# A drain behind each group of matmuls carries the semaphore update, in a four-layer graph attention kernel

## The reference

```python
def layer(x, adj, W, a, slope, bias, elu):
    wh = x @ W                                        # 4096 x 64
    e = (wh @ a[:64])[:, None] + (wh @ a[64:])[None, :]
    e = jnp.where(e > 0, e, slope * e)                # leaky relu
    att = jax.nn.softmax(jnp.where(adj > 0, e, -big), axis=1)
    h = att @ wh + bias                               # bias in layer 1 alone
    return layernorm(x + (jax.nn.elu(h) if elu else h))
```

## Time and profile before

| what | value |
|---|---|
| timed executions, median (lowest to highest) | 600.63 us (600.36 to 600.85) |
| span of the profiled execution, first to last instruction | 859.9 us |
| TensorE matmuls, busy | 419.1 us, 3453 instructions |
| TensorE weight loads, busy | 334.5 us |
| ScalarE, busy | 400.8 us |
| VectorE, busy | 349.6 us |
| GpSimd, busy | 278.0 us |
| granted TensorE clock, mean | 0.815 |

### The profile page before, as it was taken

One profiled execution on the slowest core, in us unless ns is written; L12 is line 12 of the kernel. 1 busy time (PEld: TensorE's weight loads), 2 busy tenths in 40 slices (PEclk: granted clock), 3 DMA queues, 4 the chain that ended last, 5 costly groups with the idle time before them and its releaser, 6 DMA issues.

```text
span 859.9 us, 10681 instructions
## 1 busy us (share of the span) xinstructions
PE 419.1 (49%) x3453; PEld 334.5 (39%) x3453; DVE 349.6 (41%) x1601; ACT 400.8 (47%) x876; POOL 278.0 (32%) x296
## 2 busy tenths in 40 slices
PE   2354512246655786411129983310499633104985
PEld 1243301245543675300119862210397522004964
DVE  3035813744379598200003872300048622000587
ACT  2677612555476476200325971231269612313684
POOL 0000173140320410777710034777100437771000
PEclk9999999999999998555559995755599857555997
DMA  8999962482673100222200012222000112220000
GB/s 312 428 330 428 422 198 58 173 290 100 212 282 124 17 26 27 32 27 27 27 8 2 20 30 29 28 27 27 9 1 20 34 26 27 28 28 6 8 19 28
DMA packets 20546, 84.86 MB, mean 99 GB/s; under 512 B 6083, under 2 KB 11462, under 8 KB 16262
## 3 DMA queue, kind: packets, MB, share of 16 engines
q1 hardware_dynamic: 10102, 73.15, 21.8%
q0 software_dynamic: 9344, 9.89, 9.4%
q10 hardware_dynamic: 1040, 1.08, 0.4%
HBM read 78.72 MB, written 5.37 MB: 98 GB/s over the span
## 4 chain that ended last, share of the span: by engine, by line
another core or an unknown queue 23%; PE 17%; DVE 12%; ACT 11%; issue 9%; DVEq 0%; ACTq 0%
PE bank L709 7%; ACT arena L865 4%; PE bank L689 3%; PE bank L672 3%; ACT arena L851 2%; DVE x L1313 2%; PE bank L670 1%; DVE stats L1295 1%; PE bank L705 1%; ACT arena L875 1%; DVE arena L1232 1%; ACT arena L839 1%; PE bank L574 1%; DVE res L1292 1%
## 5 line engine op out<-in xcount | busy, mean ns | idle before, releaser
L528 POOL DMA_INDIRECT xg<-table,index x292 | 277.8, 951 | 499.4 <-DMA table<-wh 299.8
L1232 DVE CUSTOM_DVE_ANT_0 arena<-bank,arena 128x256 f32<-128x256 f32 (+3 forms) x123 | 63.4, 523 | 284.7 <-ACT arena L851 224.5
L851 ACT ACTIVATE arena<-bank,sloped_own 128x256 f32<-128x256 f32 (+3 forms) x123 | 68.5, 557 | 176.3 <-remote 109.7
L689 PE MATMUL bank<-packed,arena 128*128 128x128 f32 x339 | 68.3, 323 | 120.0 <-issue 74.0
L839 ACT ACTIVATE arena<-arena,half 128x4096 bf16<-128x4096 int32 x31 | 114.7, 3703 | 19.1 <-DMA arena<-in_adj_t 18.5
L689 PEld LDWEIGHTS bank<-packed,arena 128*128 128x128 f32 x339 | 46.0, 165 | 132.7 <-issue 118.5
L875 ACT COPY arena<-bank 128x256 f32<-128x256 f32 (+3 forms) x123 | 54.1, 446 | 75.4 <-remote 55.4
L670 PE MATMUL bank<-off_row,wall 128*128 128x256 bf16 (+3 forms) x132 | 43.9, 332 | 81.2 <-issue 58.4
L709 PE MATMUL bank<-xg,arena 128*128 128x64 f32 x486 | 73.0, 284 | 10.6 <-ACT arena L875 8.6
L709 PEld LDWEIGHTS bank<-xg,arena 128*128 128x128 f32 x486 | 63.7, 197 | 24.0 <-ACT arena L875 13.5
L1029 DVE MAX8 top<-bank 128x8 f32<-128x256 f32 x31 | 13.4, 431 | 131.5 <-remote 69.5
(11 more groups left out here) (148 smaller groups left out, 780.1 us busy)
## 6 DMA issues: line engine op xcount, KB each, us to landing
arena<-in_adj_t SPq DMA_DIRECT2D x31, 2048.0 KB
xg<-table,index POOLq DMA_INDIRECT x292
table<-wh SPq DMA_DIRECT2D x24, 132.0 KB, 1.7
arena<-in_adj SPq DMA_DIRECT2D x1, 2048.0 KB, 12.9
table<-wh ACTq DMA_DIRECT2D x1, 1056.0 KB
x<-in_x SPq DMA_DIRECT2D x1, 1024.0 KB, 15.0
out_x<-x SPq DMA_DIRECT2D x8, 128.0 KB, 1.9
packed<-in_c_packed SPq DMA_DIRECT2D x1, 312.0 KB
```

Source lines behind the costliest of these rows:

```text
L528: pool.indirect_dma_start(out=xg[:, c, :], out_offset=None, in_=table[l][0:rows, :], in_offset=bass.IndirectOffsetOnAxis(ap=index[:, c:c + ...
L689: t = nc.tensor.transpose(turned_ps[turned_bank(n)][:, c * P:(c + 1) * P], scores(l, n)[:, c * P:(c + 1) * P], ident[:, :])
L851: nc.scalar.activation(scores(l, n)[:, 0:m * P], score_ps[n % len(score_ps)][:, 0:m * P], ACT.Relu, bias=sloped_own[:, k:k + 1], scale=ALP ...
L1232: nc.vector.tensor_tensor_reduce(out=y, in0=score_ps[n % len(score_ps)][:, 0:m * P], in1=y, scale=-1.0, scalar=-FLOOR, op0=ALU.add, op1=AL ...
```

## The change

In ten places of TensorE's program the matmul no longer carries the update of the group. A drain of TensorE is placed behind the group, and the drain carries it. The groups, their order, the waits in front of them, and everything on the other engines stay as they are. The transposes and products of the one-off preparation (lines 589 and 591), the overflow check and the branch for dense graphs keep their updates on the matmul.

```diff
@@ turn_rows
-                t.then_inc(xt_made, 1)
+                pe.drain().then_inc(xt_made, 1)
@@ project_rows
-                t.then_inc(wh_made, 1)
+                pe.drain().then_inc(wh_made, 1)
@@ sum_rows
                 nc.tensor.matmul(wh_ps[:, 0:F], x_total[:, :].broadcast_to([2 * F, P]), wx[:, l, 0:F],
-                                 start=True, stop=True).then_inc(sum_made, 1)
+                                 start=True, stop=True)
+                pe.drain().then_inc(sum_made, 1)
@@ pack
-                ins.then_inc(codes_made, 1)
+                pe.drain().then_inc(codes_made, 1)
@@ first_slots
-                t.then_inc(off_made, 1)
+                pe.drain().then_inc(off_made, 1)
@@ lists
-                    t.then_inc(list_made, 1)
+                    pe.drain().then_inc(list_made, 1)
@@ spread
                 for c in range(m):
-                    t = nc.tensor.matmul(bank[:, c * P:(c + 1) * P],
+                    nc.tensor.matmul(bank[:, c * P:(c + 1) * P],
                                          tcol_wide(terms[:, c1 + c, TCOL:TCOL + 1]), ident[:, :],
                                          start=False, stop=(c == m - 1), is_transpose=True)
-                t.then_inc(score_made, 1)
+                pe.drain().then_inc(score_made, 1)
@@ turn
-                t.then_inc(turned, 1)
+                pe.drain().then_inc(turned, 1)
@@ aggregate
-                t.then_inc(aggregated, 1)
+                pe.drain().then_inc(aggregated, 1)
```

More of the change, by code:

```diff
@@ L563, in turn_rows @@
                     k, at = g * GROUP + 2 * j, (n % 2 * PAIRS + j) * P
-                    t = nc.tensor.transpose(xt_ps[:, at:at + P],
+                    nc.tensor.transpose(xt_ps[:, at:at + P],
                                             x[:, k:k + 2, :].rearrange("p k f -> p (k f)"), ident[:, :])
-                t.then_inc(xt_made, 1)
+                pe.drain().then_inc(xt_made, 1)
             def project_rows(n, l, dst=wh_ps):
@@ L573, in project_rows @@
                 for j in range(PAIRS):
-                    t = nc.tensor.matmul(dst[:, 2 * j * WX:2 * (j + 1) * WX], xt[:, n % 2, j * P:(j + 1) * P],
+                    nc.tensor.matmul(dst[:, 2 * j * WX:2 * (j + 1) * WX], xt[:, n % 2, j * P:(j + 1) * P],
                                          wx_pair[:, l, :, :].rearrange("p a f -> p (a f)"), start=True, stop=True)
-                t.then_inc(wh_made, 1)
+                pe.drain().then_inc(wh_made, 1)
             def sum_rows(l):
@@ L605, in pack @@
                 for c in range(TILES):
-                    ins = nc.tensor.matmul(codes[:, c * w:(c + 1) * w], masks[:, t % 2, c * P:(c + 1) * P],
+                    nc.tensor.matmul(codes[:, c * w:(c + 1) * w], masks[:, t % 2, c * P:(c + 1) * P],
                                            packer[:, :], start=False, stop=(c == TILES - 1))
-                ins.then_inc(codes_made, 1)
+                pe.drain().then_inc(codes_made, 1)
             def first_slots(b):
@@ L616, in first_slots @@
                 pe.wait_ge(deg_made, b + 1)
-                t = nc.tensor.matmul(room_ps[:, 0:n], before[:, :], degb[:, 0:n], start=True, stop=True)
+                nc.tensor.matmul(room_ps[:, 0:n], before[:, :], degb[:, 0:n], start=True, stop=True)
                 if k0 < PARTED:
                     nc.tensor.matmul(room_ps[:, n:2 * n], before[:, :], degb[:, n:2 * n], start=True, stop=False)
-                    t = nc.tensor.matmul(room_ps[:, n:2 * n], ones_b[:, :], degb[:, 0:n], start=False, stop=True)
-                t.then_inc(off_made, 1)
+                    nc.tensor.matmul(room_ps[:, n:2 * n], ones_b[:, :], degb[:, 0:n], start=False, stop=True)
+                pe.drain().then_inc(off_made, 1)
             def lists(b):
@@ L640, in lists @@
                             high = k < PARTED and place < HIGH_TO[k]
-                            t = nc.tensor.matmul(dst, off_row[:, at:at + P], rows, start=False,
+                            nc.tensor.matmul(dst, off_row[:, at:at + P], rows, start=False,
                                                  stop=(k == tiles[-1] and not high))
@@ L646, in lists @@
                                 nc.tensor.matmul(dst[:, w - 1:w], ones_b[:, :], less, start=False, stop=False)
-                                t = nc.tensor.matmul(dst[:, w - 1:w], off_high[:, at:at + P], less,
+                                nc.tensor.matmul(dst[:, w - 1:w], off_high[:, at:at + P], less,
                                                      start=False, stop=(k == tiles[-1]))
-                    t.then_inc(list_made, 1)
+                    pe.drain().then_inc(list_made, 1)
             def spread(l, q):
@@ L688, in turn @@
                 for c in range(m):
-                    t = nc.tensor.transpose(turned_ps[turned_bank(n)][:, c * P:(c + 1) * P],
+                    nc.tensor.transpose(turned_ps[turned_bank(n)][:, c * P:(c + 1) * P],
                                             scores(l, n)[:, c * P:(c + 1) * P], ident[:, :])
-                t.then_inc(turned, 1)
+                pe.drain().then_inc(turned, 1)
             def aggregate(l, q):
@@ L708, in aggregate @@
                 for c in range(m):
-                    t = nc.tensor.matmul(agg[:, at:at + F], slots(l, n)[:, c * P:(c + 1) * P],
+                    nc.tensor.matmul(agg[:, at:at + F], slots(l, n)[:, c * P:(c + 1) * P],
                                          wh[:, c0 + c, 0:F] if k == DENSE else xg[:, FIRST[k] + c0 + c, 0:F],
```

## The result

The changed kernel takes 924.89 us (median of 4 runs, 923.14 to 926.07) against 600.74 us of the kernel before: 1.538 times as long, with a 95% interval of 1.535 to 1.542. The forecast was 706 us, with a range from 632 to 790.

What follows compares the result with a forecast made beforehand. TensorE was taken to bound the burst, with gathers close as a bound. Drains would add 89 us in layers 1 to 3, 13 in layer 0 and 3 ahead of it: 600.6 + 105 = 706 us, range 632 to 790.

Steps and rivals of the forecast that it cites:

- The clock, the rival that was given 0.07: Bursts of layers 1 to 3: TensorE's clock falls to 1.2 GHz, some 33 us more a layer, 805 us; chance 0.07.
- the sum: Whole kernel: drain costs less slack, 89 us in layers 1 to 3, 13 + 3 before, 706 us; chance 0.74.
- against it: Argument against the clock rival: clock 1.00 throughout the light rounds, with weight loads in 21.14 of 27.50 us.
- b: Cost of one drain between two TensorE groups without a gap: 0.34 us, from 0.17 to 0.50.
- The estimate by the 12 ns: One drain on TensorE taken at 12 ns: b would be 0.28 us, the sum some 22 us less.
- The slack of the rounds: Rounds from 460.7 to 505.0 us: slack between 1.3 and 8.3 us, taken as 4.8, set against 88 drains.
- Layer 0: From 290 to 343 us, some 80 drains less 14 us of slack cost 13 us; drains ahead of 290 us, 3.
- the long releases: ScalarE starts 11 us after line 672 while gathers are issued; taken as the profiler's, hardly present in timed executions.
- Gathers cover it: Timed layers bound by the gathers' pace, hiding 20 us of drains a layer: 646 us; chance 0.11.
- Faster by releases that are no longer held: Matmul updates are held while gathers are issued, a drain's are not: 555 us at best, about 580 with half; chance 0.05.
- Nothing changes: The last matmul's update already comes so late that a drain between groups adds nothing: 601 us; chance 0.03.
- The sign of a clock under 0.9: In the profile after, a clock under 0.9 from 453 us to the burst's end would speak for the clock rival.

Runs made afterwards that it cites:

- single kinds: Kernel before with only one of aggregates (line 709), turns (line 689) or spreads (lines 670, 672) drained: 642.43, 627.85 and 625.31 us.
- two kinds: Kernel before with turns and aggregates drained: 824.93 us, 775.44 with repeated matmuls added; with spreads and aggregates drained: 830.57 us.
- the new trace: The kernel before, unchanged, run once more with a profile: 602.71 us, span 600.8 us.
- aggregates alone: Kernel before with only the 164 updates of the aggregates (line 709) carried by a drain: 642.43 us.
- turns alone: Kernel before with only the 164 updates of the turns (line 689) carried by a drain: 627.85 us.
- spreads alone: Kernel before with only the 164 updates of the spreads (lines 670 and 672) carried by a drain: 625.31 us.
- layer 0 alone: Drains only in the listing and in layer 0, 204 of 609, the rest as in the kernel before: 660.17 us.
- the fill without drains: Kernel before, no drains, each transpose of a turn done twice and a spread's first matmul three times, into the same place: 653.29 us.

## Why the prediction failed

**The clock, the rival that was given 0.07.** It is the main error in kind: the sum had no term for it. The rounds did run at the lower clock, and by the estimate above it costs 109 to 143 us in layers 1 to 3 and a part of the 59 us of layer 0. The price was set at 99 us (805 - 706) for three layers, a little low, with nothing for layer 0. A sign of layer 0 stood in the rows: the weight loads of 0.333 us that gave the price lie at 190 to 218 us, where the clock column of that trace reads 1.00. What was wrong is the step "against it": the clock was 1.00 in the light rounds at 21.14 us of weight loads in 27.50, and from this one stretch without drains I concluded that it would stay up with drains. For light rounds with 1.0 us of matmuls in 2.1, as my own sum had them, no row stood. Nor was the question asked whether the clock, which is at 0.52 early in a layer in any case, would come back among drained rounds; in the changed kernel it did not. The rows at hand could not exclude this, and the chance should have been a third or more. The mechanism was cited from the Trainium skill, TensorE: Matmul & The Clock Gate, section on a second HAM failure mode. The runs agree in part: there are short idles between groups (0.23 us) with a low clock beside them, but not a swing, as the clock is 0.50 from 380 to 530 us without a break.

**The price of one drain.** b was 0.34 us, measured 0.38 at the upper clock and 0.43 at the lower. Two of its three terms are confirmed: the tail of the last matmul (0.16 us taken and measured) and the drain's own time (0.07 taken, 0.079 measured). The third, the weight load that is no longer hidden, was taken at 0.11; what is left of the 0.23 us for it is 0.15, and it was not measured by itself. The estimate by the 12 ns of the Trainium skill, VectorE: DVE Perf Modes, section on the DRAIN you can't avoid, would have been further off: the measured drain with nothing to wait for costs 79 ns.

**The slack of the rounds.** In layers 1 to 3 the sum has 89 us, against 118 to 152 us for the drains at the upper clock. The larger b makes 0.04 x 404 = 16 us more. The stages of the sum hold 8 + 7 + 8 + 88 + 14 = 125 drains, where a layer has 140: 15 were left out, at most 15 x 0.38 = 6 us a layer. The rest is slack that I set against the drains: 1.6 us among the turns and 4.8 us in the rounds of a layer, the half price in the tail and next to nothing for the spreads of tile 0. Which of these was worst was not separated. The single kinds cost 0.15 to 0.25 us a drain, so a part of the first gap is hidden, and about as much as the forecast had it (89 / 404 = 0.22 us). With two kinds at the upper clock it is 59 to 93 us for 246 drains in layers 1 to 3, 0.24 to 0.38 us, and with all kinds 0.29 to 0.38.

**Layer 0.** 13 + 3 us were forecast, 59 measured. The listing was right in kind (3 forecast, 5 to 7 measured). The rest is in the rounds from 290 to 343 us and ahead of them. There the sum took 14 of the time without weight loads for room, and it took the upper clock for granted. In the changed kernel these rounds ran at the lower one, as the durations show. How the 52 us are shared between the clock and the room that was not there was not separated.

**Reading the stretched execution.** That the long releases aren't in the timed executions was right, and the price of a layer that followed was near: 93 us by the rows, 98.0, 99.2 and 111.6 in the new trace, with layer 0 at 292 instead of 321. That they are the profiler's was wrong as a rule: in all 15 others the span is 2 us under the time, also where matmuls carry the updates while gathers are issued (aggregates alone, turns alone, spreads alone, layer 0 alone, the fill without drains). Why that one execution was longer stays open.

**The other rivals.** Gathers cover it: in the kernel before a layer is 98 us with 73 gathers at 1.25 us in it (91 us), but from 350 to 390 us TensorE's matmuls are busy for 38.57 us of 40, so it was TensorE that bounded the end of the layer. No run shows a cover of 20 us a layer: aggregates alone cost 32 us in layers 1 to 3, of the 47 us that 123 drains at 0.38 us make, so some 15 us were hidden in three layers, by whatever it was. Faster by releases that are no longer held: the releases weren't held, and who carries the update makes 0.1%. Nothing changes: no.

**The signs named ahead.** For the 64 matmuls of tile 0, some 10 us were expected, and they took 16 (the first starts at 401.7, the last at 417.6 us); for a heavy round 2.8 us, and one from 441.50 to 445.99 us took 4.49. The sign of a clock under 0.9 was the one that came. ScalarE did start within 0.3 us behind the spreads of tile 0, which was to speak for the held release, but it does so in the kernel before too (0.03 us), so this sign could not tell the cases apart.

## What to carry to other kernels

Leave the semaphore update on the last matmul; a drain is no free place for it, since it ends the overlap of one group with the next: 0.38 to 0.43 us where nothing hides it, and 0.15 to 0.25 us on average with one drained kind. In a kernel whose TensorE works in groups of 2 to 8 small matmuls, ask what new gaps do to the clock as well as what they cost themselves: one gap in a round cost 24 to 41 us, and the turns' gap on top of the aggregates' cost 183 us more, because it also cost the clock (by the estimate 113 to 147 us of the 224 for the two together). Read the clock from the durations of equal matmuls (0.27 or 0.42 us here) as well as from the column: in layer 0 the two disagree. And where a profile's span isn't the kernel's time, take it again before a stage is explained by it.

## What was not expected of the hardware

A kernel can get faster by matmuls that do nothing: 780 more of them took 37 us off (887.81 against 924.89 us), 49 us in the case of two kinds, by bringing the clock of layers 1 to 3 from 0.53 to 0.56 up to 0.85 to 0.92. The clock column of a trace can read 1.00 for 351 us in which every turn takes 417 ns or more, the duration of the lower level. A drain on TensorE is seen in the profile with a duration of up to 3.1 us, most of which is its group's matmuls and not its cost. And one profiled execution of the kernel before had the updates of matmuls delayed by 11 us while gathers were issued, which no other execution showed.
